# The end of a decoder layer: two of four last roots moved off GpSimd, the last dense step tile by tile, and all gathers issued in one row

## The reference

```
h = gelu(einsum('bsd,edh->besh', an, re_w1) + re_b1[None, :, None, :])
routed = einsum('bse,besh,ehd->bsd', gates, h, re_w2) + einsum('bse,ed->bsd', gates, re_b2)
x = x + (shared + routed + an + attn_out)
m = mean(x, axis=-1); v = var(x, axis=-1)
x = (x - m) / sqrt(v + 1e-05)
```

## Time and profile before

| what | us |
|---|---|
| median of 3 runs | 904.88 |
| lowest and highest | 903.38 and 906.44 |
| the profiled execution: its time | 905.01 |
| the profiled execution: its span, first to last instruction | 903.2 |

### The profile page before, as it was taken

One profiled execution on the slowest core, in us unless ns is written; L12 is line 12 of the kernel. 1 busy time (PEld: TensorE's weight loads), 2 busy tenths in 40 slices (PEclk: granted clock), 3 DMA queues, 4 the chain that ended last, 5 costly groups with the idle time before them and its releaser, 6 DMA issues.

```text
span 903.2 us, 17391 instructions
## 1 busy us (share of the span) xinstructions
PE 803.7 (89%) x5325; PEld 531.4 (59%) x5325; DVE 689.0 (76%) x2494; ACT 572.8 (63%) x1445; POOL 561.5 (62%) x638
## 2 busy tenths in 40 slices
PE   5899999998789999999899999999988889893864
PEld 2344444444567677775466766766665568881643
DVE  4788888888879888899788599689949835651756
ACT  3678877884689999997566475476535653540324
POOL 5888888887641333333777496577969786437151
PEclk9899999999999999999999999999999999997888
DMA  8300000000051111001222122212222444532011
GB/s 235 109 1 0 1 1 0 1 1 0 1 135 54 54 53 43 2 2 48 53 69 68 48 55 65 68 40 59 76 59 59 132 150 132 174 108 53 4 36 47
DMA packets 57851, 51.88 MB, mean 57 GB/s; under 512 B 11586, under 2 KB 43042, under 8 KB 57762
## 3 DMA queue, kind: packets, MB, share of 16 engines
q1 hardware_dynamic: 55394, 46.05, 18.4%
q0 software_dynamic: 2304, 4.72, 1.8%
q10 hardware_dynamic: 64, 0.02, 0.0%
HBM read 21.66 MB, written 12.32 MB: 38 GB/s over the span
## 4 chain that ended last, share of the span: by engine, by line
PE 50%; POOL 19%; DVE 13%; issue 8%; ACT 5%; another core or an unknown queue 4%; ACTq 0%; DVEq 0%; POOLq 0%
PE psum L2028 5%; PE psum L2199 4%; DVE area L1482 4%; PE psum L2061 4%; POOL area L970 4%; PE psum L2045 3%; PE psum L2336 3%; PE psum L2355 3%; PE psum L2394 3%; PE psum L2087 3%; POOL area L879 3%; PE psum L2258 3%; PE psum L2372 2%; POOL slot_in L958 2%
## 5 line engine op out<-in xcount | busy, mean ns | idle before, releaser
L970 POOL TENSOR_TENSOR area<-area,rinv 128x512 f32<-128x512 f32 x64 | 94.2, 1472 | 69.2 <-DVE rinv L1803 68.8
L1275 ACT ACTIVATE area<-area,negmax 128x128 f32<-128x128 f32 (+1 forms) x256 | 112.8, 444 | 17.9 <-DVE negmax L1482 17.0
L1122 ACT ACTIVATE area<-area,negmax 128x256 f32<-128x256 f32 x256 | 108.8, 505 | 0.3
L1482 DVE CUSTOM_DVE_ANT_0 area<-psum,area 128x256 f32<-128x256 f32 x256 | 93.2, 420 | 17.6 <-PE psum L2013 16.8
L1470 DVE SCALAR_TENSOR_TENSOR area<-psum,ccol,cs 128x512 f32<-128x512 f32 x128 | 89.4, 740 | 21.1 <-PE psum L2061 20.9
L1482 DVE CUSTOM_DVE_ANT_0 area<-psum,maskc 128x128 f32<-128x128 f32 (+1 forms) x256 | 75.8, 351 | 9.8 <-issue 5.5
L2028 PE MATMUL psum<-ident,area 128*128 128x128 f32 x512 | 70.9, 279 | 9.1 <-DVE area L1522 7.6
L2061 PE MATMUL psum<-area,qkw 128*128 128x512 f32 x128 | 71.7, 642 | 7.7 <-DVE area L1470 5.0
L1777 DVE SCALAR_TENSOR_TENSOR ntok<-psum,gate,ntok 128x128 f32<-128x128 f32 x140 | 39.4, 343 | 44.8 <-remote 30.5
L2028 PEld LDWEIGHTS psum<-ident,area 128*128 128x128 f32 x512 | 56.9, 142 | 18.5 <-issue 11.1
L1265 ACT ACTIVATE area<-psum 128x512 f32<-128x512 f32 x32 | 19.1, 597 | 75.6 <-PE psum L2394 67.5
(11 more groups left out here) (308 smaller groups left out, 2120.5 us busy)
## 6 DMA issues: line engine op xcount, KB each, us to landing
area<-area SPq DMA_DIRECT2D x256, 64.0 KB
slot_out<-area SPq DMA_DIRECT2D x17, 256.0 KB, 2.3
area<-slot_in SPq DMA_DIRECT2D x8, 512.0 KB, 4.1
slot_in<-gate SPq DMA_DIRECT2D x5, 768.0 KB, 4.6
area<-in_L_ffn_re_w SPq DMA_DIRECT2D x14, 256.0 KB
area<-in_mask_BxSxS_ik SPq DMA_DIRECT2D x8, 256.0 KB, 3.6
area<-in_L_attn_W SPq DMA_DIRECT2D x5, 256.0 KB, 6.1
area<-in_x SPq DMA_DIRECT2D x4, 256.0 KB, 3.5
```

The costliest lines, as they stand in the source:

```text
L970: pool.tensor_tensor(p4, p4, rinv[:, u % 4, 0:4].unsqueeze(2).to_broadcast([128, 4, w]), ALU.mult)\
L1122: last = act.activation(P[:, n % 4, r, mm, :], P[:, n % 4, r, mm, :], ACT.Exp, bias=negmax[:, n % 4, r, mm:mm + 1], scale=-1.0)
L1275: last = act.activation(Pc[:, u % 4, r, mm, 0:w], Pc[:, u % 4, r, mm, 0:w], ACT.Exp, bias=negmax[:, u % 4, r, mm:mm + 1], scale=-1.0, accu ...
L1482: return nc.vector.tensor_tensor_reduce(out=dst, in0=scores, in1=mask, scale=1.0, scalar=HIGHEST, op0=ALU.add, op1=ALU.min, accum_out=low)
```

## The change

- GpSimd issues the gathers of the groups 0, 1 and 2 in one row. The root of group 0, which stood between those of group 1 and those of group 2, now comes behind all of them.
- The roots of the groups 2 and 3 are no longer GpSimd's. ScalarE takes the square root of variance plus epsilon for the four tiles of a group (`last_deviation`), VectorE the reciprocal and the shift (`last_rstd`). A square root on a constant is put behind the last GELU, so that the table of the function is loaded there.
- In the last step (k = 51) the four output tiles go to four banks, each with a semaphore increment of its own, and VectorE adds them one by one, with the reciprocal and shift of group 2 and the statistics of group 3 in between.
- `combine(8)` is done one step earlier.

```diff
-                         DENSE_K + 26: 6, DENSE_K + 28: 7, DENSE_K + 30: 8}
+                         DENSE_K + 26: 6, DENSE_K + 28: 7, DENSE_K + 29: 8}
+        LAST_BANK = (bank[2 + (len(STEPS) - 1) % 2], bank[4], bank[5], bank[6])
+        LAST_ORDER = (("add", 0), ("rstd", 2), ("negmean", 2), ("add", 1), ("add", 2), ("add", 3), ("rstd", 3), ("negmean", 3))
+        LAST_DONE = {what: i + 1 for i, what in enumerate(LAST_ORDER)}
...
-            for g in range(2):
+            for g in range(3):
                 for j in range(3):
                     gather(g, j)
-            last_root(0, 0)
-            for j in range(3):
-                gather(2, j)
-            for i, g in enumerate(NORMS[1:]):
-                last_root(i + 1, g)
+            for i in range(2):
+                last_root(i, NORMS[i])
...
             def last_apply(i, g, tiles):
-                act.wait_ge(s_rs, NG + 2 * i + 2)
+                if i < 2:
+                    act.wait_ge(s_rs, NG + 2 * i + 2)
+                else:
+                    act.wait_ge(l_a, LAST_DONE["negmean", i])
...
+            def last_deviation(i, g):
+                act.wait_ge(s_mv, NG + i + 1)
+                act.activation(sdev[:, i - 2, :], mv[:, g, :, 1], ACT.Sqrt, bias=eps_o[:, 0:1]).then_inc(s_ss, 1)
+
+            act.activation(sdev[:, 2, :], eps_o[:, 0:TPG], ACT.Sqrt)
             for i, g in enumerate(NORMS):
+                if i >= 2:
+                    last_deviation(i, g)
                 last_apply(i, g, range(TPG) if i < 3 else range(2, TPG))
...
+            def last_rstd(i, g):
+                dve.wait_ge(s_ss, NG + i - 1)
+                nc.vector.reciprocal(rstd[:, g, :], sdev[:, i - 2, :]).then_inc(l_a, 1)
+                dve.wait_ge(l_a, LAST_DONE["rstd", i])
+                nc.vector.scalar_tensor_tensor(mneg[:, g, :], mv[:, g, :, 0], -1.0, rstd[:, g, :], ALU.mult, ALU.mult)\
+                    .then_inc(l_a, 1)
+
+            def last_add(q):
+                k = len(STEPS) - 1
+                n = (NG - 1) * TPG + q
+                dve.wait_ge(m_a, k)
+                dve.wait_ge(m_y, k + q + 1)
+                nc.vector.scalar_tensor_tensor(res[:, n, :], LAST_BANK[q][:, 0:D], gate[:, n, STEPS[k][1]:STEPS[k][1] + 1],
+                                               res[:, n, :], ALU.mult, ALU.add).then_inc(l_a, 1)
+
+            def last_tile_stats(q):
+                dve.wait_ge(l_a, LAST_DONE["add", q])
+                nc.vector.bn_stats(st[:, NG - 1, q, :], res[:, (NG - 1) * TPG + q, :]).then_inc(s_st, 1)
...
-            dve.wait_ge(m_a, len(STEPS))
-            last_stats(3, 3)
-            dve.wait_ge(s_rs, NG + 2 * 3 + 1)
+            last_add(0)
+            last_rstd(2, 2)
+            last_add(1)
+            last_tile_stats(0)
+            last_add(2)
+            last_tile_stats(1)
+            last_add(3)
+            last_tile_stats(2)
+            last_tile_stats(3)
+            last_moments(3, 3)
+            last_rstd(3, 3)
...
-                        last = nc.tensor.matmul(bank[2 + p][:, i * D:(i + 1) * D], h, we2[:, :] if e == E else experts[:, e, 1, :],
-                                                start=True, stop=True)
+                        dst = LAST_BANK[i][:, 0:D] if k == len(STEPS) - 1 else bank[2 + p][:, i * D:(i + 1) * D]
+                        last = nc.tensor.matmul(dst, h, we2[:, :] if e == E else experts[:, e, 1, :], start=True, stop=True)
+                        if k == len(STEPS) - 1 and i < TPG - 1:
+                            last.then_inc(m_y, 1)
```

More of the change, by code:

```diff
@@ L177, in program @@
         ssm = sb("ssm", [128, 2, NT])
+        sdev = ssm[:, 0, 0:3 * TPG].rearrange("p (g t) -> p g t", t=TPG)
         sse = sb("sse", [128, 2, NT])
@@ L341, in program @@
         s_vbb = sem("v_bias_loaded")
-        s_ss = sem("square_sums_done")
+        s_ss = sem("square_sums_then_last_deviations_done")
         s_rms = sem("rms_steps_done")
@@ L380, in program @@
         m_y = sem("expert_output_done")
+        l_a = sem("last_vector_step_done")
         m_a = sem("expert_output_added")
@@ L1841, in last_stats, with last_moments @@
                     nc.vector.bn_stats(st[:, g, q, :], res[:, g * TPG + q, :]).then_inc(s_st, 1)
+                last_moments(i, g)
+            def last_moments(i, g):
                 dve.wait_ge(s_st, TPG * (NG + i) + TPG)
@@ L1845, in last_stats @@
                 last.then_inc(s_mv, 1)
-            for k in range(1, len(STEPS)):
+            def last_rstd(i, g):
[14 more added lines that the diff above has]
+                nc.vector.bn_stats(st[:, NG - 1, q, :], res[:, (NG - 1) * TPG + q, :]).then_inc(s_st, 1)
+            for k in range(1, len(STEPS) - 1):
                 if slot_batch(k + 2) is not None:
```

## The result

| | before | after |
|---|---|---|
| median, us | 904.49 (9 runs) | 907.43 (9 runs) |
| lowest and highest | 902.64 and 906.44 | 906.05 and 909.79 |
| the profiled execution | 905.01 | 907.24 |
| its span | 903.2 | 905.5 |

The ratio is 1.0034, with an interval from 1.0022 to 1.0046: slower by 3.1 us (2.0 to 4.2). The total is close to the forecast, but the rows will show that two of its terms were wrong, in opposite directions.

What follows compares the result with a forecast made beforehand. Bound taken: dense steps nearly standing still while gathers are in flight, TensorE's signals arriving late. Row of gathers +2.2 and end +0.1 make +2.3 us on 905.0: 907.3, median 907.2; range 903.6 to 910.0.

Steps and rivals of the forecast that it cites:

- What bounds the kernel: Last 104 us: while rows of gathers are in flight, TensorE's signals reach ScalarE and VectorE late; dense steps nearly stand still.
- The rival that ties it to places in the program: Standstills belong to program places, not to gathers; the one row moves nothing, 905.1 us; chance 0.20.
- The row of gathers, +2.2: Joining GpSimd's gathers in one row loses 12.6 us more in the first standstill and saves 10.4: +2.2 us.
- in 15.0 us that is 1.4 steps: Dense steps passing in the first standstill's added 15.0 us, at one in 10.9 us; worth 2.4 us.
- the second row's 10.4: Loss around the second row of gathers, 857 to 889 us, which was to go: 10.4 us.
- upper bound of 4.6: Cost of the one row if no step passes in the added 15.0 us: +4.6 us.
- nothing gets through: No step passes in the added 15 us of standstill: +4.6 + 0.1, 909.7 us; chance 0.22.
- The end's work, +0.1: After the last steps: earlier statistics -0.4, VectorE's wait +1.3, reciprocal and shift +0.3, last root -1.1; together +0.1 us.
- The sum: Row of gathers and end together +2.3 us on the profiled 905.0: 907.3, or 907.2 for the median.
- One row costs less than two: Late signals get through more often in the added stretch; with 6 steps net -5.9 us, 899.1; chance 0.12.
- ScalarE's switch costs its drain: At the end, the table switch costs a drain too, or VectorE's alternations cost: +1.5 instead of +0.1, 908.6; chance 0.06.
- VectorE's alternations: In the last step, seven alternations between tile additions and other work: 0 forecast, +0.3 us if each pays some 0.05 us.

Runs made afterwards that it cites:

- e1: Kernel before with only GpSimd's order changed: all 36 gathers in one row, root of group 0 behind them; 912.58 us, ratio 1.0060.
- e2: Changed kernel with the old GpSimd order: 24 gathers, root of group 0, 12 gathers, root of group 1; 903.87 us, ratio 0.9964 to before.
- e8: The changed kernel unaltered, run again on a quick chip; 863.63 us against 867.92 us for the kernel before, ratio 0.9967.
- e11: The kernel before with only the gathers put in one row, run again on a quick chip; 867.82 us, ratio 1.0005.

## Why the prediction was right, and where it was wrong

**What bounds the kernel.** Right. Where the standstill occurs at all, it stands where gathers are in flight. The rival that ties it to places in the program gave 905.1, and it has fallen: full pace near 870 after the change, one step from 838 to 856 in e1 where before there was a restart, two standstills again in e2. That it is the signal that comes late, as I read it, fits the order on TensorE: after the change it had gone on to the matmuls of 835.51 and 837.38 when the GELU for the hidden layer of 822.10 was still 16 to 20 us off. (The profile's ends of matmuls are modelled, so the order says more than the distance.) Before, the last two hidden layers of the first standstill were 21.2 and 13.8 us ahead of their GELUs, and those of the second up to 8.6. In e8 and e11 no GELU from 800 us on starts more than 0.3 us after its hidden layer ends. The Trainium skill's sentence that "DMA never contends with a compute engine" (SBUF: State Buffer, "Who interferes with whom") agrees with the rows of both kinds of chip as far as an instruction's own length goes: the GELU takes 0.69 us on either. Of signals the sentence says nothing, and it was a signal that came late, so the rival could not rest on it.

**The row of gathers, +2.2.** This step failed in its size, at "in 15.0 us that is 1.4 steps". Counted in steps again, before lost 22.0 us from 812 to 838 (26 less 2.3 times 1.75) and 1.5 in the restart from 838 to 857 (19 us with 6.88 / 0.687 = 10.0 steps, the row below), 23.5 together. After lost 39.1 from 812 to 862 (50 less 6.2 times 1.75). That is 15.6 more, where I had 12.6; less the second row's 10.4 it is +5.2. Where the 3 us come from, to half a microsecond: no step in the added 15 us instead of 1.4 (2.4 us), and a longer way back, 5.8 us from the last gather's end at 850.0 to the next GELU at 855.8 instead of 2.6 (3.2 us); against it 0.7 step more ahead of 838 (1.2 us) and a shorter restart (0.9 us). Timed alone the row costs +5.4 us (3.9 to 7.1); its middle lies above even the upper bound of 4.6, which the interval still holds. This is the rival "nothing gets through". A mean rate over two standstills was the wrong choice: the first let its steps pass early, so the added part should have been priced by its late part, which the earlier trace rows showed as empty. The stretch of the kernel before that the forecast took as unchanged:

```profile
838.00:857.00 19.00, 6.88 (x11) 0.87 0.00 1
```

**The end's work, +0.1.** Right, and nearly term by term. Table load 1.28 us (forecast 1.28) and the small root straight behind it, no drain on ScalarE. The statistics of group 2 start 2.67 us after the last GELU's start, 0.5 sooner than before (0.4 forecast). VectorE's wait 1.32 (1.3). Moments' end to ScalarE's last application 0.77 us (901.12 to 901.89; 0.75 forecast, 1.82 before). All in all 8.82 us against 8.80: 0.0 for +0.1.

**The sum left out what comes behind the last application.** It started from the span of before and moved its end as much as the last application. But 5.3 us lay there, and GpSimd's DRAIN was their cause. Taking GpSimd's last root away was priced by what waits for the root; its second effect, that GpSimd ends 9 us sooner instead of last, was not priced. It is worth -2.6 us in the traces, which lies within the -3.3 us (-2.0 to -4.5) of the end timed alone; the remaining 0.7 is not resolved.

**The two errors cancel**: +4.81 + 0.02 - 2.57 = +2.26 in the traces, the very number forecast. That is luck: a row of gathers mis-sized by 2.6 us, and a term of the same size and the other sign that was not in the sum. The median of 907.43 does not support the way it was reached.

**The rivals.** "One row costs less than two" fell: no pace of a step in 3.5 us was ever seen inside a standstill. "ScalarE's switch costs its drain" fell: the activation follows the load within 0.01 us, in all fourteen executions. Nor do VectorE's alternations cost: the first tile and the rest down to the end of the moments take 0.32 + 2.06 us, against 2.42 before.

**What stays open.** Why what TensorE signals arrives late in some comparisons while gathers are in flight, and whether fewer gathers, paced ones or plain transfers would avoid it. The three kernels made for that never met a chip that shows it. Whether it belongs to the chip or to its condition at the time isn't known either. Of five comparisons two had a kernel before at 904.5 and 907.6 us and three at 867.4 to 867.9, with nothing between; the last four ran on four different chips, and which chip the first ran on is not known.

## What to carry to other kernels

A program isn't over with its last useful instruction: look at what lies between it and the end of the span, and at which engine is the last to finish. In these runs a GpSimd that issued more indirect transfers had the longer DRAIN, and so would have to be through with its own work the earlier. Taking the last work off GpSimd gained more than all the reordering of roots around it. A stretch that stands still is to be priced by its own late part and not by a mean. And before work is rearranged around a standstill, run the kernel before on a second chip: here the same change is 3 us slower on one and 3 us faster on the other.

## What the hardware showed that was not expected

- GpSimd closes with a DRAIN of 6.21 us (6.20 to 6.21 in the eight executions with 72 indirect transfers, 5.23 with 60, 3.27 with 36), as long after a last transfer 38 us back (after: gathers until 850.0, DRAIN at 887.9) as in the others. At 6.21 us it sets the end here as soon as it starts later than 3.7 us before the last application's end (after: SyncE was through at 905.27, less 6.21 is 899.06; the applications end at 902.77).
- The same kernel takes 904 to 908 us on some chips and 867 to 868 on others. The two traces of the changed kernel are 43.9 us apart in span. 38.5 of it lie behind the first gather, which is what its standstill loses (39.1 by steps); of the other 5.4, 1.3 were there at 656 us, and 4.2 more by 675. In between the first chip's trace has its only earlier wait for "remote", 8.2 us that end at 667.58, while GpSimd was issuing indirect transfers (the scatters, 642.0 to 672.2); the quick chip's has none. The timeline of the changed kernel, first chip:

```profile
660.15 1.01 POOL L963 DMA_INDIRECT slot_in<-xT,area  x1 [0.17 <-issue]
...
667.58 0.60 ACT L1267 ACTIVATE area<-psum 128x512 f32<-128x512 f32 x1 [8.20 <-remote]
```

- TensorE's granted clock stayed at 1.00 through the gathers on the quick chips. On the other it was, in the changed kernel, at 1.00 from 812 to 819, 0.95 to 826 and 0.50 to 838, with GELUs at 813.74, 819.34 and 834.77 alone: it fell after the steps had all but stopped.
